# A graph layer's gathers and scatters on GpSimd's queue, two units at a time instead of one, in another order of the edge tiles

## The reference, cut to what matters

```python
xs = node_feats[:, :32] @ W_up0 / 32 ** 0.5                 # 50000 nodes, 128 features each
xv = einsum('nmc,mk->nkc', node_feats[:, 32:], W_up1) / 32 ** 0.5
ss, vv = xs[senders], xv[senders]                            # 50000 edges gather their sender
w = MLP(radial_embedding(edge_length)).reshape(-1, 4, 32)    # 8 -> 64 -> 64 -> 128, silu
mid_s, mid_v = products of w, ss, vv and the edge's direction
msg = segment_sum(mid, receivers, num_segments=50000)        # added up by receiver
out = msg @ W_out / ... / 16
x = layernorm(x + out)
```

## Time and profile before

| | |
|---|---|
| runs, median (lowest, highest) | 1280.47 us (1278.93, 1281.45) |
| the profiled execution's own time | 1277.2 us |
| its span, first to last instruction | 1275.0 us |
| TensorE's granted clock, mean | 0.857 |
| busy: POOL, PE, DVE, ACT | 80%, 71%, 54%, 42% |
| indirect DMAs on POOL | 392 gathers, 392 scatters |
| moved | 130.5 MB, 102 GB/s in the mean |

### The profile page before, as it was taken

How to read it: one execution, slowest core, us unless ns; L and a number is a source line. 1 busy time by engine, 2 the same in 40 slices (tenths; PEclk the granted TensorE clock), 3 DMA queues, 4 the chain that set the end, 5 groups by cost and what they waited for, 6 DMA issues and landing times.

```text
span 1275.0 us, 25680 instructions
## 1 busy us (share of the span) xinstructions
PE 902.3 (71%) x6206; PEld 840.5 (66%) x6206; DVE 692.1 (54%) x2889; ACT 536.2 (42%) x1404; POOL 1016.4 (80%) x818
## 2 busy tenths in 40 slices
PE   1799768676877777767776767777767777767740
PEld 1799657665766676667676767666657776767640
DVE  5766434564665465556465456366556455646331
ACT  5345223444354355345444444435435524544411
POOL 7788778788888788888788888888888888888885
PEclk7899888998888888888888988888888788888785
DMA  5787884444444443543552453444444354354343
GB/s 157 196 188 187 189 183 70 94 69 97 93 97 93 97 93 68 122 97 40 135 108 42 93 123 66 97 93 97 93 97 93 73 118 95 40 129 87 70 62 59
DMA packets 82644, 130.54 MB, mean 102 GB/s; under 512 B 16168, under 2 KB 66859, under 8 KB 81328
## 3 DMA queue, kind: packets, MB, share of 16 engines
q0 software_dynamic: 68992, 51.43, 31.4%
q1 hardware_dynamic: 12936, 77.36, 17.3%
q10 hardware_dynamic: 680, 1.38, 0.3%
HBM read 78.40 MB, written 77.31 MB: 122 GB/s over the span
## 4 chain that ended last, share of the span: by engine, by line
POOL 45%; issue 30%; DMA 22%; POOLq 1%; DVE 0%; SPq 0%; ACTq 0%; ACT 0%
POOL acc L459 27%; DMA acc<-msg,index 21%; POOL sender L437 18%; DMA sender<-in_x_dram,index 1%; POOLq L443 0%; DMA len_raw<-in_edge_weight_dram 0%; POOLq L458 0%; POOLq L457 0%; POOLq L445 0%; DMA total<-acc 0%; POOLq L444 0%; POOL vec_raw L396 0%; POOLq L452 0%; ACTq L264 0%; DVE low_raw L768 0%
## 5 line engine op out<-in xcount | busy, mean ns | idle before, releaser
L459 POOL DMA_INDIRECT acc<-msg,index x392 | 627.1, 1600 | 121.7 <-issue 117.3
L437 POOL DMA_INDIRECT sender<-in_x_dram,index x392 | 382.2, 975 | 123.4 <-issue 101.9
L940 DVE TENSOR_TENSOR wts<-ps_wts,bias 128x512 f32<-128x512 f32 x98 | 67.8, 692 | 417.6 <-PE ps_wts L546 417.6
L530 PE MATMUL ps_hid<-hid,mlp 128*128 128x256 f32 x196 | 86.5, 531 | 265.4 <-ACT hid L674 265.4
L559 PE MATMUL ps_sum<-same,mid 128*128 128x128 f32 x1568 | 251.8, 314 | 0.7 <-DVE mid L955 0.7
L559 PEld LDWEIGHTS ps_sum<-same,mid 128*128 128x128 f32 x1568 | 244.0, 229 | 10.5 <-DVE mid L955 0.8
L530 PEld LDWEIGHTS ps_hid<-hid,mlp 128*128 128x128 f32 x196 | 36.5, 233 | 282.3 <-ACT hid L674 282.3
L659 ACT COPY msg<-ps_msg 128x128 f32 (+1 forms) x98 | 26.1, 266 | 454.2 <-DMA acc<-msg,index 444.4
L571 PE MATMUL ps_msg<-outw,sumT 128*128 128x64 f32 x1568 | 186.5, 272 | 1.2 <-ACT sumT L650 1.2
L571 PEld LDWEIGHTS ps_msg<-outw,sumT 128*128 128x128 f32 x1568 | 182.8, 192 | 1.4 <-ACT msg L660 1.4
L711 ACT ACTIVATE normed<-total,shift,rstd 128x128 f32 x392 | 157.3, 481 | 36.4 <-DVE shift L1005 32.2
(11 more groups left out here) (139 smaller groups left out, 1058.9 us busy)
## 6 DMA issues: line engine op xcount, KB each, us to landing
acc<-in_x_dram SPq DMA_DIRECT2D x80, 312.5 KB
total<-acc SPq DMA_DIRECT2D x30, 832.0 KB, 4.7
out_dram<-normed SPq DMA_DIRECT2D x29, 832.0 KB
sender<-in_x_dram,index POOLq DMA_INDIRECT x392, 3.0
acc<-msg,index POOLq DMA_INDIRECT x392, 3.3
out_dram<-normed ACTq DMA_DIRECT2D x1, 832.0 KB
vec_raw<-in_edge_attr_dram SPq DMA_DIRECT2D x1, 576.0 KB
acc<-zeros SPq DMA_DIRECT2D x1, 320.0 KB, 4.0
```

Of the source, the lines that this page charges most:

```text
L437: pool.indirect_dma_start(sender[:, u % SRING, i, :], None, x, bass.IndirectOffsetOnAxis(ap=index[:, u, 0, i:i + 1], axis=0)).then_inc(her ...
L459: pool.indirect_dma_start(acc, bass.IndirectOffsetOnAxis(ap=index[:, v, 1, i:i + 1], axis=0), msg[:, v % RING, i, :], None, compute_op=ALU.add
L530: pe.matmul(ps_hid[:, 2:4, :], mlp1[:, :], hid0[:, k % 2, :], start=True, stop=True).then_inc(hid1_ps, 1)
```

## The change

1. Behind the first two units, four units share four rows: unit w of the group takes quarter w of each of the four rows. The first two units stay as they were. `turns` and `row_tiles` now work in five parts instead of two.
2. `BATCH = 2`: POOL's queue has the gathers of units v + 6 and v + 7, and then the scatters of units v and v + 1. Both numbers of `scatter_orders` are loaded ahead of the gathers.
3. From unit 2 on scatter n waits for the landing of scatter n - 4; the flag now looks at three tiles before it instead of two, so the table has a third distance.

```diff
+BATCH = 2
...
         def turns(a, w):
 
-            return a.rearrange("p (j w) (r q) -> p w q j r", w=2, r=2)[:, w]
+            if w == G:
+                return a[:, 0:2, :].rearrange("p w (r q) -> p r w q", q=2)
+            return a[:, 2:UNITS, :].rearrange("p (j w) r -> p w j r", w=G)[:, w]
 
         def row_tiles(a, w):
 
-            return a[:, w:w + 3:2, 0:UNITS].rearrange("p q (j r) -> p q j r", r=2)
+            if w == G:
+                return a[:, :, 0:2].rearrange("p (q w) r -> p r w q", w=2)
+            return a[:, w, 2:UNITS].rearrange("p (j r) -> p j r", r=G)
+
+        PARTS = (G, 0, 1, 2, 3)
...
-            def scatters(v):
-
-                order = pool.value_load(scatter_orders[0:1, v:v + 1], min_val=2, max_val=2 * PIECES - 1)
+            def order_of(v):
+
+                return pool.value_load(scatter_orders[0:1, v:v + 1], min_val=2, max_val=2 * PIECES - 1)
+
+            def scatters(v, order):
+
...
-                    if n >= 3:
-                        pool.wait_ge(*landed(n - 3))
-                    for of in (n - 2, n - 1) if i == 0 else (n - 1,):
+                    far = 3 if v < 2 else 4
+                    if n >= far:
+                        pool.wait_ge(*landed(n - far))
+                    for of in range(n - far + 1, n) if i == 0 else (n - 1,):
...
-            for v in range(UNITS):
-                if v + LAG < UNITS:
-                    gathers(v + LAG)
-                scatters(v)
+            for v in range(0, UNITS, BATCH):
+                orders = [order_of(u) for u in range(v, v + BATCH)]
+                for u in range(v + LAG, min(v + LAG + BATCH, UNITS)):
+                    gathers(u)
+                for u in range(v, v + BATCH):
+                    scatters(u, orders[u - v])
...
-            for w in range(2):
+            for w in PARTS:
                 mm = dve.tensor_copy(turns(index[:, 0:UNITS, 0, :], w), row_tiles(ps_src, w))
...
-                for apart in range(1, 3):
-                    n = TILES - apart
-                    dve.tensor_tensor(meet[:, apart - 1, apart:TILES], hi[:, 0:n], lo[:, apart:TILES], ALU.is_ge)
-                    mm = dve.tensor_tensor(meet_too[:, apart - 1, apart:TILES], hi[:, apart:TILES], lo[:, 0:n], ALU.is_ge)
+                spans = [(apart, apart if apart < 3 else 2 * G) for apart in range(1, 4)]
+                for apart, first in spans:
+                    dve.tensor_tensor(meet[:, apart - 1, first:TILES], hi[:, first - apart:TILES - apart],
+                                      lo[:, first:TILES], ALU.is_ge)
+                    mm = dve.tensor_tensor(meet_too[:, apart - 1, first:TILES], hi[:, first:TILES],
+                                           lo[:, first - apart:TILES - apart], ALU.is_ge)
```

More of the change, by code:

```diff
@@ L63 @@
 RSQRT_BITS = float(0x5f3759df)
-assert UNITS % 2 == 0 and LAG <= SRING and (UNITS - 2) % SRING == 0 and UNITS <= P and FULL == UNITS - 1 and FULL >= 96
+assert UNITS % 2 == 0 and LAG <= SRING and UNITS % BATCH == 0 and (UNITS - 2) % G == 0 and (UNITS - 2) % SRING == 0 and UNITS <= P and FULL == UNITS - 1 and FULL >= 96
 assert NORM_AFTER > STATS_AFTER and NORM_AFTER > RING // 2 and (UNITS - 2) % RING == 0 and CHUNKS % 2 == 0 and PIECES % 2 == 0 and N % PIECE == 0 and N - CHUNK - (CHUNKS - 1) * STEP in range(REST + 1)
@@ L115, in bass_gnn @@
         high = sb("high", [1, UNITS, G])
-        meet = sb("meet", [1, 2, TILES])
-        meet_too = sb("meet_too", [1, 2, TILES])
+        meet = sb("meet", [1, 3, TILES])
+        meet_too = sb("meet_too", [1, 3, TILES])
         piece_int = sb("piece_int", [1, UNITS], I32)
@@ L494, in _ @@
             pe.wait_ge(act_planes, 4)
-            pe.wait_ge(prepared, 3)
+            pe.wait_ge(prepared, 2)
             pe.wait_ge(index_in, 1)
@@ L695, in unit @@
                     msg_out(u - 1, k - 1)
-            act.wait_ge(prepared, 4)
+            act.wait_ge(prepared, 3)
             act.wait_ge(act_pre, 2)
@@ L774, in _ @@
             dve.wait_ge(planes, 2)
-            for w in range(2):
-                dve.tensor_copy(turns(dst_all[:, :, :], w), row_tiles(ps_dst, w)).then_inc(prepared, 1)
+            for w in PARTS:
+                mm = dve.tensor_copy(turns(dst_all[:, :, :], w), row_tiles(ps_dst, w))
+            mm.then_inc(prepared, 1)
             dve.wait_ge(ends_ps, 2)
-            for w in range(2):
+            for w in PARTS:
                 dve.tensor_scalar(turns(low[:, :, :], w), row_tiles(ps_high[0:1, :, :], w), -1.0, float(N - 1),
@@ L785, in _ @@
             dve.tensor_copy(dump_rowf[:, :], dump_row[:, :]).then_inc(dump_ready, 1)
-            dve.wait_ge(prepared, 2)
+            dve.wait_ge(prepared, 1)
             dve.wait_ge(dump_ready, 1)
@@ L822, in make_scatter_orders @@
                 lo, hi = (a[:, :, :].rearrange("p v i -> p (v i)") for a in (low, high))
-                for apart in range(1, 3):
-                    n = TILES - apart
-                    dve.tensor_tensor(meet[:, apart - 1, apart:TILES], hi[:, 0:n], lo[:, apart:TILES], ALU.is_ge)
-                    mm = dve.tensor_tensor(meet_too[:, apart - 1, apart:TILES], hi[:, apart:TILES], lo[:, 0:n], ALU.is_ge)
+                spans = [(apart, apart if apart < 3 else 2 * G) for apart in range(1, 4)]
[4 more added lines that the diff above has]
+                                           lo[:, first - apart:TILES - apart], ALU.is_ge)
                 link(mm)
-                for apart in range(1, 3):
-                    mm = dve.tensor_tensor(meet[:, apart - 1, apart:TILES], meet[:, apart - 1, apart:TILES],
-                                           meet_too[:, apart - 1, apart:TILES], ALU.mult)
+                for apart, first in spans:
+                    mm = dve.tensor_tensor(meet[:, apart - 1, first:TILES], meet[:, apart - 1, first:TILES],
+                                           meet_too[:, apart - 1, first:TILES], ALU.mult)
                 link(mm)
-                link(dve.tensor_tensor(meet[:, 0, :], meet[:, 0, :], meet[:, 1, :], ALU.max))
+                for apart in (1, 2):
+                    link(dve.tensor_tensor(meet[:, 0, :], meet[:, 0, :], meet[:, apart, :], ALU.max))
                 link(dve.tensor_reduce(meet_unit[:, :], meet[:, 0, :].rearrange("p (v i) -> p v i", i=G), AX_X, ALU.max))
```

## The result

The changed kernel takes **1269.06 us** in the median of four runs (1267.58 to 1270.71), beside 1280.35 (1278.93 to 1281.45) for the kernel before: a ratio of 0.9908, with a 95% interval of 0.9893 to 0.9922. The prediction was 1266.6, within 1259 to 1275; of the forecast gain of 13.9 us 11.3 came. Measured a second time, beside other experiments, the changed kernel had a ratio of 0.9895 (0.9878 to 0.9911). The profiled execution took 1267.58 us with a span of 1265.8, which is 9.2 less than the span before (1275.0); TensorE's mean clock was 0.842.

A forecast was written before the change was run, and what follows sets the result against it. POOL, a closed chain with 0.30 us between indirect DMAs, was taken to bound the kernel. Terms -8.0, -4.6, -1.5, -0.5, +0.25 and +0.5 sum to -13.85 us, taking 1280.5 to 1266.6 us, range 1259 to 1275.

The forecast's parts named there:

- What bounds the kernel: POOL's queue: a closed chain working back to back, with a floor of 0.30 us between two indirect DMAs.
- Fewer changes of kind: POOL's queue: 46 runs of each kind instead of 92, saving 0.11 us per gather change, 0.06 per scatter change: -8.0 us.
- rival B: Surplus of a run's first instructions comes from VectorE and the sequencer at that moment, so it stays: 1274.6 us; chance 0.08.
- Where VectorE blocks a scatter: VectorE's product at L951 lengthens some twenty-five POOL scatters; the new distance halves the toll: -4.6 us, bounds -9.2 and +25.1.
- Rival A: POOL's switches go, VectorE's collisions stay or grow up to twofold: 1271.2 us, or 1280.4 with twice the toll; chance 0.14.
- Fourth scatter instead of third: POOL's scatters wait on the 4th ahead; the old wait rarely bites: -1.5 us, bounds 0 and -3.5.
- First scatter: At the start, four more gathers before scatter 0 cover the lateness of message 0: -0.5 us.
- Two order loads ahead of the gathers: Sequencer loads two orders under a run's last scatters, so they cost 0; without cover 74 us, one bare 37.
- Preparation: Before POOL's first gather, VectorE copies the indices in three more instructions over the same columns: +0.25 us.
- Conflict flags: Flagged units make each scatter wait for its predecessor's landing; no flag is set before or now: 0.
- The end: Behind the last scatter, the last full chunk's later store delays the store of the rest rows: +0.5 us, bounds 0 and +3.
- the inference that was weighed: Two-SBUF-input tensor_tensor would not stall descriptor generation; the L951 surplus may stay, its term nought, the time that of rival A.

The follow-up runs named there:

- the pair without most of the blocking: Changed kernel and kernel before, each with product and count taking one input from PSUM, every row to spare rows: 1262.99 us (0.9854) and 1271.59 us (0.9916).
- the third-scatter kernel: The changed kernel, but every scatter waits for the 3rd one ahead instead of the 4th: 1276.11 us, ratio 0.9947.
- the late kernels: Changed kernel with each unit's order loaded ahead of its own scatters: runs of seven units 1350.48 us; runs of four 1409.15 us, once more 1396.41 us.

## Why the prediction was right, and where it was off

- **What bounds the kernel**: right. In every undisturbed profile POOL's idle time between its first gather and its last scatter is 0.30 us a piece, with 2 to 10 us in all above that.
- **Fewer changes of kind, -8.0 us**: the mechanism is right and the gathers' 0.11 us too; the scatters' 0.06 was too small and measured 0.10, so the term is 9.4 in POOL's busy time, just past the bound of 9 (8.6, give or take 2, in the medians of the pair without most of the blocking). My 1.56 for a scatter in a long run was a mean over 21; the floor from the fourth on is 1.552, and the first two of a run cost 0.10 above it together. With one unit at a time this gain is gone, with nothing but runs of two units it is there; rival B, that the surplus belongs to the moment and not to the change of kind, falls.
- **Where VectorE blocks a scatter, -4.6 us**: the mechanism held (take the second SBUF input away and 11.3 us go from the kernel before), but the working was wrong and the size is not settled. In the two profiled executions the toll fell by 0.2 in all and by 1.8 behind 50 us. The medians say more: without most of the blocking the kernel before loses 11.3 us and the changed one 4.9. That is 6.4 us of difference (5.5 by the ratios), give or take some 3. A likely reason that the two don't agree, not shown, is that the only profile of before is of an execution 3 to 6 us faster than that kernel's medians. So the term lies between -0.2 and about -6, and -4.6 may have been right. What the traces do show wrong is the reason, "I expect chance meetings at half of today's toll". The new distance is just as fixed as the old, and I had looked at one instruction, the product at L951, and at scatters. The shorter instructions behind it (L972, L923) also have two SBUF inputs, and a run of gathers lying where VectorE works takes hits of 0.10 us at the same place, 31 times in 46. Rival A had the collisions at their old size and gave 1271.2; the result lies between it and the forecast.
- **Fourth scatter instead of third, -1.5 us**: wrong as it was put. In the kernel one unit at a time the new order and wait together are worth 1.8 us (0.4 to 3.2, by the ratio's interval). The gaps rose from 2.8 to 5.1 us, but by one of 4.2 ahead of the first scatter; among the scatters behind it they fell from 1.8 to 0.9. Under runs of two units the third scatter, with the new tiles, costs 5 us. I had asked whether the old wait bites in the old queue, not whether it would in the new one, where a second unit's scatters follow without gathers between them. With the old tiles the gaps are as large (9.7 us beside 8.6), but the ratio is 0.9910 and not 0.9947. How much of the cost hangs on the tiles is open: 2.3 us of it here are the end's.
- **First scatter, -0.5 us**: it moved. No scatter before 60 us waits, but two behind it, at 62.90 and 65.55, have gaps of 0.74 and 1.10, 1.2 us over the floor; the second ended with a landing. Another of 1.29 us stands among the gathers, at 46.63.
- **Two order loads ahead of the gathers, 0**: right; no run of gathers begins with a gap over 0.30.
- **Preparation, +0.25 us**: +0.24 (11.95 for 11.71).
- **Conflict flags, 0**: right; the largest gap before a scatter of the changed kernel is 1.10 us, where a flag costs 2.2 on each of four.
- **The end, +0.5 us**: -0.2; the two transfers passed each other, by luck of the phase, as the third-scatter kernel with its 2.3 us shows.

By the traces the sum is -9.4 - 0.2 + 0.3 + 0.24 - 0.2 = -9.3 us, against -9.6 between the profiled executions' own times and -13.85 forecast: 4.4 us were missing at VectorE and 2.3 at waits and the first scatter, the changes of kind brought 1.4 more and the end 0.7. Between the medians it is -11.3, and -15.0 the second time (1282.84 to 1267.86). What the median execution of before spent more than the profiled one, no profile shows; the experiment without two SBUF inputs points at blocking. So part of the near hit is luck: between the two profiled executions the forecast missed by 4.2 us, between the medians by 2.5.

As for the inference that was weighed, that a tensor_tensor with two SBUF inputs would not stall descriptor generation (the Trainium skill, SBUF — State Buffer, Who interferes with whom): the runs speak against it for indirect DMAs, and for the same section's statement that it contends with GpSimd's reads. The surplus at L951 and L968 goes when one input moves to PSUM.

## What to carry to other kernels

Where a queue is a closed chain, first count what comes with each change of kind of its work and test a longer run of one kind alone; here an edit of the queue alone had nearly all of the gain. A collision of two engines in fixed phase does not thin out when the phase changes: list every instruction that can collide, not only the one seen to do so, and lay each over the new phase. Price a wait in the queue that the change makes, not in the one that is there. And before a trace is taken as the measure of a term, look where its own execution lies among the others: here the one before was faster than all of them, and one term of the sum can't be sized for it.

## What had not been expected of the hardware

A VectorE instruction with two SBUF inputs lengthens an indirect DMA of GpSimd by what is left of it when the DMA starts, less 0.12 us, for gathers as for scatters, if it has a lead of 0.04 us. In the profiles of the kernel before and of the changed one, 37 DMAs that started less than 0.03 us behind such an instruction were none the longer. Ahead of the steady state the long ones count most. Timeline of the changed kernel:

```profile
18.61 1.38 DVE L811 TENSOR_TENSOR vec_sq<-vec_all 128x1176 f32<-128x1176 f32 x1
18.68 2.13 POOL L444 DMA_INDIRECT sender<-in_x_dram,index  x1 [0.30 <-issue]
```

19.99 - 18.68 - 0.12 = 1.19, and the gather took 2.13 in place of 0.94. Such hits ahead of 50 us come to 1.7 us in the profile of the kernel before and to 2.4 to 3.5 in all others, and no run has tried to take them away.

POOL's first two DMAs of a kind cost more than the rest: scatters 1.62 and 1.58 before 1.56 and 1.55, gathers 1.02 and 0.98 before 0.94. The prediction had this surplus from the means, without a reason; there is none yet. Two candidates fall by the durations in the runs of seven and of four units and with the old tile order. A scatter inside a run is back at 1.55 when it follows a gap of over 1 us (the median of 105 with the old order, of 49 and 44 in the two with four units), so it is not the pause; and so is the first of each unit inside a run, ahead of which the late kernels load an order number, so it is not the load.
